# A two-layer graph network on one core: prologue and tail rearranged

## What is computed

```
h = relu(layernorm(x))
Wh = h @ W.T + b_W ;  s_s = Wh @ a_src ;  s_d = Wh @ a_dst
e  = leaky_relu(s_s[src] + s_d[dst] + a_b)          # softmax of e over the edges of one dst
h' = sum over edges of attn * Wh[src]  +  h @ res_W.T + res_b
x  = x + gru(h', h)                                  # layer 0
h  = relu(layernorm(x))
4 times:  a[dst] += W_edge[type] @ h[src] + b_edge[type] ;  h = gru(a, h)
x  = x + h
```

## Time and profile before

| | us |
|---|---|
| median of 3 runs | 586.27 |
| all runs | 581.45 to 586.57 |
| the profiled execution | 584.53 |
| its span on the core | 582.7 |
| busy: PE, DVE, ACT, POOL | 478.6, 267.2, 183.3, 34.2 |

### The profile page before, as it was taken

The page is one execution under the profiler, slowest core; times in us unless marked ns, Lnnn a source line. Parts: engine busy times, 40 slices in busy tenths (PEclk is TensorE's granted clock), DMA queues, the critical chain, the costliest instruction groups (busy, mean ns, idle before and its releaser), DMA issues.

```text
span 582.7 us, 9927 instructions
## 1 busy us (share of the span) xinstructions
PE 478.6 (82%) x3672; PEld 385.0 (66%) x3672; DVE 267.2 (46%) x618; ACT 183.3 (31%) x291; POOL 34.2 (6%) x50
## 2 busy tenths in 40 slices
PE   0146887687777779779659999899998999999995
PEld 0024453454555559769338889788997889888893
DVE  6793888888888883204720122302222122302224
ACT  0042005546576675213241222212222122312221
POOL 2560010000001100000100000000000000000000
PEclk9998988899999999979759999999999999999998
DMA  6000000000000000000000000000000000000001
GB/s 159 1 0 0 1 0 1 2 1 1 1 2 1 1 1 3 3 3 1 0 5 1 0 1 2 1 1 1 1 1 3 1 1 1 1 1 1 1 1 44
DMA packets 5846, 3.65 MB, mean 6 GB/s; under 512 B 499, under 2 KB 5640, under 8 KB 5796
## 3 DMA queue, kind: packets, MB, share of 16 engines
q1 hardware_dynamic: 3188, 1.76, 1.2%
q10 hardware_dynamic: 2608, 1.19, 0.8%
HBM read 2.31 MB, written 0.64 MB: 5 GB/s over the span
## 4 chain that ended last, share of the span: by engine, by line
PE 62%; DVE 19%; issue 7%; DVEq 5%; ACT 3%; POOL 2%; DMA 1%; SPq 0%; POOLq 0%; ACTq 0%
PE big L1259 29%; DVE cell_hot L717 6%; PE small L1269 6%; PE big L1038 4%; PE big L1080 4%; DVE exp_a L756 2%; DVE absent L739 2%; DVEq L254 2%; PE small L1148 2%; PE small L1142 2%; PE small L1146 2%; PE small L1147 2%; PE small L1144 2%; PE small L1143 2%; ACT hn L398 1%
## 5 line engine op out<-in xcount | busy, mean ns | idle before, releaser
L1259 PE MATMUL big<-nibbles,store 128*128 128x256 fp8e4 (+1 forms) x1624 | 180.2, 272 | 6.7 <-DVE store L910 3.4
L1259 PEld LDWEIGHTS big<-nibbles,store 128*128 128x128 f16 x1624 | 159.5, 99 | 25.3 <-issue 7.5
L1038 PE MATMUL big<-cell_hot,store 128*128 128x320 bf16 x420 | 77.9, 321 | 26.1 <-DVE cell_hot L717 25.3
L717 DVE TENSOR_SCALAR cell_hot<-iota,cell_w,fields 128x640 bf16<-128x640 f16 x210 | 77.7, 440 | 19.4 <-PEq L1109 8.7
L1038 PEld LDWEIGHTS big<-cell_hot,store 128*128 x420 | 36.3, 103 | 67.4 <-issue 54.4
L565 ACT ACTIVATE store<-big 128x1024 f32<-128x1024 f32 x20 | 20.5, 1025 | 106.3 <-PE big L1259 106.3
L910 DVE SCALAR_TENSOR_TENSOR store<-small,store 128x256 f16<-128x256 f32 x20 | 8.5, 424 | 91.3 <-ACT store L570 91.1
L806 DVE SCALAR_TENSOR_TENSOR store<-store 128x256 f32<-128x256 f32 x25 | 10.6, 425 | 76.0 <-ACT store L511 76.0
L1269 PE MATMUL small<-store,wT 128*128 128x256 f32 x160 | 37.8, 379 | 0.0
L509 ACT ACTIVATE store<-small,gb 128x256 f32<-128x256 f32 x22 | 10.4, 474 | 73.4 <-PE small L1148 73.4
L1269 PEld LDWEIGHTS small<-store,wT 128*128 128x128 f32 x160 | 28.8, 190 | 3.2
...
## 6 DMA issues: line engine op xcount, KB each, us to landing
...
```

The lines of the kernel that those rows point to most:

```text
L717: last = v.tensor_scalar(cell_hot[:, slot], iota[:], cell_w[:, half, bass.ds(tile + slot, 1)], fields[:, 1, bass.ds(tile + slot, 1)], ALU. ...
L1038: last = mm(big[:, 2 * half + b, 0:HALF], lane_hot[:, bass.ds(tile + slot, 1)].rearrange("p a l -> p (a l)"), cell_hot[:, slot, b * HALF:( ...
L1259: last = mm(big[:, q + t // 2, (t % 2) * CH:(t % 2) * CH + w], h16[parity][:, i, part], A8[:, t % 2, i, c * CH:c * CH + w, t // 2], start= ...
```

## The change

- `Wh` and the destination scores come from one product of each feature tile with `w_gat` (W turned, and one more column W^T a_dst), the bias added by a matmul of one row. The constants are folded from `proj`. The source scores (`score_rows`) are made by PE after the first window.
- All weights are transposed in the prologue, before the features, and ACT copies them before its `hn`.
- `var_e` and all `cell_w` are made by DVE; POOL keeps the power. `bn_stats` is put ahead of the `table`.
- `table` holds one number per window (first tile and number of tiles); "tiles before" is summed in registers. DVE loads the registers of two windows after `weigh`, no longer before it.
- The matmul that ends a window has 2 columns, not 320.
- `degrees`: block 0 after the last window, block 1 before the flag, block 2 before the last two `nodes_turn`, blocks 3 to 9 after the first GRU. The check of the counts comes before the last `weigh`, and the last two turns move across the branch.

```diff
-        def edge_tiles(eng, j):
-            return (eng.value_load(table[0:1, 0, j:j + 1]),
-                    eng.value_load(table[0:1, 1, j:j + 1]),
-                    eng.value_load(table[0:1, 2, j:j + 1], min_val=0, max_val=SLOTS))
+        def edge_tiles(eng, j, ahead):
+            word = eng.value_load(table[0:1, j:j + 1], min_val=0, max_val=256 * (ETP + 1))
+            first, tiles = eng.snap(word & 255), eng.snap(word >> 8)
+            return (first, tiles, ahead), eng.snap(ahead + tiles)
...
-            return big[0:TYPES, 2 + n // 4 % 2]
+            return big[0:TYPES, (2, 1, 0)[(n + 2) // 4]]
...
-            def window_cells(j, half):
-                if later(j, 2):
-                    pool.wait_ge(K.window, j - 1)
-                g.tensor_tensor(cell_w[:, half], fields[:, 2],
-                                base_w[:, bass.ds(j, 1)].to_broadcast([P, ETP]), ALU.subtract).then_inc(K.cellw, 1)
...
-                g.tensor_tensor(var_e[:], mv[:, :, 1], eps[:], ALU.add).then_inc(S0.var, 1)
                 pool.wait_ge(S0.var, r + 1)
...
-            pool.wait_ge(S0.fields, 2)
-            for j in range(NW):
-                window_cells(j, j % 2)
...
-            def weights(k):
+            act.wait_ge(S0.w_T, 1)
...
+            act.wait_ge(S0.proj_ps, 1)
+            a.copy(proj[:], psA[:, 0:4]).then_inc(S0.proj, 1)
+            act.wait_ge(S0.proj, 1)
+            act.wait_ge(L.ab, 16)
+            a.copy(w_gat[:, P:P + 1], proj[:, 1:2])
+            a.activation(dst_bias[:], proj[:, 3:4], ACT.Identity, bias=ab_col[:, 0:1])
+            a.activation(a_rows[:], ones[:], ACT.Copy, scale=proj[:, 0:1]).then_inc(S0.folded, 1)
+            for k in range(4):
                 act.wait_ge(S0.w_T, 2 + k)
-                a.copy(wT[:, 2 + 4 * k:6 + 4 * k], big[:, k % 2].rearrange("p (m o) -> p m o", o=P)
-                       ).then_inc(S0.w_sb, 1)
-            act.wait_ge(S0.w_T, 1)
...
+            turn(0)
             act.wait_ge(S0.s_ps, 1)
...
+            a.activation(s_rows[:], smallf[:, 0:NP], ACT.Identity, bias=proj[:, 2:3]).then_inc(S0.s_rows, 1)
+            for J in range(1, NT + 2):
                 turn(J)
-            weights(0)
-            weights(1)
-            degrees(0, 4)
-            turn(NT + 1)
...
-            degrees(8, 10)
+            degrees(0, 2)
...
             with act.If(1 - flag):
+                turn(NT + 2)
                 first_cells(lambda: attn_out(NT - 1, NT - 1))
+            degrees(2, 6)
+            degrees(6, 10)
...
             link(v.tensor_tensor(tmp_i[:, 1], tmp_i[:, 1], tmp_i[:, 2], ALU.bitwise_or))
             v.scalar_tensor_tensor(fields_r[:, 2], win_r, float(CELLS), tmp_i[:, 1], ALU.mult, ALU.add)
...
...
+                if j >= 2:
+                    dve.wait_ge(K.pair, ends[j - 2])
+                v.tensor_scalar(cell_w[:, half], fields[:, 2], -float(CELLS * j), None, ALU.add).then_inc(K.cellw, 1)
+            variances(0)
+            dve.wait_ge(S0.best_T, 1)
...
+            link(v.tensor_scalar(rg_f[:, 1], down, -1.0, 2.0 * P, ALU.mult, ALU.add))
...
             dve.wait_ge(S0.fields, 2)
...
                 v.tensor_tensor(lane_hot[:, k:k + part],
                                 iota[:, 0:P].unsqueeze(1).to_broadcast([P, part, P]),
                                 fields[:, 0, k:k + part].unsqueeze(2).to_broadcast([P, part, P]),
                                 ALU.is_equal).then_inc(S0.lanes, 1)
-                if k == 0:
...
-                link(v.tensor_tensor(gb[:, l, 0:2], bcol[:, gi:gi + 2], bcol[:, gh:gh + 2], ALU.add))
...
+                for l, (gi, gh) in enumerate(((B_GI, B_GH), (B_IH, B_HH))):
+                    link(v.tensor_tensor(gb[:, l, 0:2], bcol[:, gi:gi + 2], bcol[:, gh:gh + 2], ALU.add))
...
+            def next_range(j):
+                if j < NW:
+                    ranges[j], ends[j] = edge_tiles(dve, j, ends[j - 1])
             def turn(J):
                 if there(J):
                     one_hots(2 * J, 0, ranges[2 * J])
                 if there(J - 1):
                     read_digits(J - 1)
-                for j in (2 * J + 1, 2 * J + 2):
-                    if j < NW:
-                        ranges[j] = edge_tiles(dve, j)
+                if there(J + 1):
+                    window_cells(2 * J + 2, 0)
                 if there(J - 2):
                     weigh(J - 2)
+                next_range(2 * J + 1)
+                next_range(2 * J + 2)
                 if there(J):
                     one_hots(2 * J + 1, 1, ranges[2 * J + 1])
                 if there(J - 1):
                     row_max(J - 1, J - 1)
+                if there(J + 1):
+                    window_cells(2 * J + 3, 1)
                 if there(J - 3):
                     reciprocals(J - 3)
-            ranges = {0: edge_tiles(dve, 0)}
+            dve.wait_ge(S0.table, 1)
+            ranges, ends = {}, {-1: 0}
...
+                if J == 0:
+                    gate_biases()
             dve.wait_ge(K.counted, NT)
...
             with dve.If(1 - flag):
+                turn(NT + 1)
...
-            pe.wait_ge(S0.table, 1)
-            pe.wait_ge(S0.fields, 2)
...
+                pe.wait_ge(s, 16)
+            for k in range(4):
+                for m in range(4):
+                    last = t_.transpose(big[:, k, m * P:(m + 1) * P], wn[:, 2 + 4 * k + m], ident[:])
+                last.then_inc(S0.w_T, 1)
+            pe.wait_ge(S0.bias_sb, 1)
+            pe.wait_ge(S0.b_cols, 1)
+            mm(psA[:, 0:2], wn[:, W_GAT], bcol[:, A_SRC:A_DST + 1], start=True, stop=True, skip_group_check=True)
+            mm(psA[:, 2:4], b_cols[:], bcol[:, A_SRC:A_DST + 1], start=True, stop=True,
...
-            pe.wait_ge(S0.w_sb, 1)
-            for lo, hi in spans():
-                last = mm(smallf[:, lo:hi], wT[:, W_GAT], hT[:, lo:hi], start=True, stop=True)
-            last.then_inc(S0.WhT_ps, 1)
-            pe.wait_ge(S0.WhT, 1)
-            pe.wait_ge(S0.bias_sb, 1)
+            pe.wait_ge(S0.folded, 1)
...
-                mm(psD[:, i:i + 1], WhT[:, i * P:(i + 1) * P], bcol[:, A_DST:A_DST + 1], start=True, stop=True,
-                   skip_group_check=True)
-            pe.wait_ge(S0.a_rows, 1)
...
-            last.then_inc(S0.s_ps, 1)
...
-                last = t_.transpose(smallf[:, i * P:(i + 1) * P], WhT[:, i * P:(i + 1) * P], ident[:])
...
+                o = small[:, i // 3, i % 3 * (P + 1):(i % 3 + 1) * (P + 1)]
+                mm(o, hT[:, i * P:(i + 1) * P], w_gat[:], start=True, stop=False, skip_group_check=True)
+                last = mm(o[:, 0:P], ones[0:1, :], brow[B_W:B_W + 1], start=False, stop=True, skip_group_check=True)
+            last.then_inc(S0.Wh_ps, 1)
...
+            def score_rows():
+                pe.wait_ge(S0.Wh, 1)
+                pe.wait_ge(S0.s_dst, 1)
+                for lo, hi in spans():
+                    last = mm(smallf[:, lo:hi], a_rows[:], hT[:, lo:hi], start=True, stop=True)
+                last.then_inc(S0.s_ps, 1)
...
-                    last = mm(big[:, 2 * half + b, 0:HALF], zero16[:, 0:P], zero16[:], start=False, stop=True,
+                    last = mm(big[:, 2 * half + b, 0:2], zero16[:, 0:P], zero16[:, 0:2], start=False, stop=True,
...
+                else:
+                    pe.wait_ge(S0.s_rows, 1)
...
-                    window(2 * J, 0, edge_tiles(pe, 2 * J))
+                    next_window(2 * J, 0)
+                if J == 0:
+                    score_rows()
...
-            pe.wait_ge(C.const, 7 + TYPES)
-            pe.wait_ge(S0.Wh, 1)
-            pe.wait_ge(S0.s_dst, 1)
...
+            pe.wait_ge(S0.w_sb, 5)
...
-            for s in (L.w2, L.w3, L.w4, L.w5, L.w6):
-                pe.wait_ge(s, 16)
-            weights(0)
-            weights(1)
-            count_turn(NT - 1)
-            aggregate(NT - 3)
-            degrees(0, 4)
-            prob_turn(NT - 2, NT)
-            weights(2)
-            weights(3)
-            degrees(4, 8)
-            aggregate(NT - 2)
+            degrees(0, 1)
+            turn(NT)
             pe.wait_ge(V.total, 1)
-            pe.wait_ge(S0.w_sb, 4)
             mm(big[:, 0, 0:2], ones[:], total[:], start=True, stop=True,
                skip_group_check=True).then_inc(V.total_ps, 1)
-            prob_turn(NT - 1, NT)
-            degrees(8, 10)
+            aggregate(NT - 2)
+            degrees(1, 2)
...
-            def first_cells(after_first):
+            def first_cells(before_first, after_first):
                 residual(0)
                 residual(1)
-                pe.wait_ge(K.degsb, 3)
-                pe.wait_ge(K.probsb, NT)
+                before_first()
+                pe.wait_ge(K.degsb, 1)
                 for c in range(NCH):
                     gates(0, c, c, c % 2, back=2 * (c >= 2))
                     if c == 0:
                         after_first()
+                        pe.wait_ge(K.probsb, NT)
                     if c + 2 < NCH:
```

(5 more changed lines are left out.)

142 lines of the change are left out of this document (70 added, 72 removed).

## The result

The changed kernel took **556.0 us** (median of 4 runs, 555.5 to 556.6), the kernel before beside it 585.8: ratio 0.951, 95% interval 0.946 to 0.955. Forecast were 551.2 us and a range of 544 to 561. Both spans are of one profiled execution, 582.7 and 554.5 us. The table cuts them at the same five events (the end of the last window is that of its last product with `cell_hot`); "sum" is the shift so far.

What follows compares the result with a forecast made beforehand. It saw everything decided in the first 300 us, bound by prologue chains, then DVE in the windows, then PE in the tail. Terms -13.3 - 0.7 - 9.4 - 21 + 11.1 = -33.3 from 584.53 gave 551.2 us, range 544 to 561.

Steps and rivals of the forecast that it cites:

- Part 1: Prologue: first window product at 43.3 us against 56.62, -13.3 us, with DVE's first `cell_hot` at 42.0.
- part 3: Turns 1 to 9: fewer loads, placed behind a multiplication, remove the 1.80 us pause before `weigh`; -9.4 us.
- part 4: Last window to first gates: 320 degree matmuls, weight transposes and a wait leave PE's path; -21 us.
- part 5: Behind the first GRU: degree blocks 3 to 9 stand in front of everything; +11.1 us.
- C: Rival: cheaper tail, PE stays at 2.4 GHz into the steps and part 4's waits are short; 546 us, chance 0.08.
- E: Rival: slower than before, PE left at 1.2 GHz in the four steps; 596 us at 90 us of it, chance 0.03.
- F: Rival: prologue's gain not kept, an unseen wait holds PE before the features; part 1 gives -3, 561 us, chance 0.04.
- A: Rival: in the turns DVE's loads stay open, not hidden under the multiplication; +11, 562 us, chance 0.08.
- D: Rival: degrees come back whole behind the GRU, at clock 0.50 with cold transposes; +6, 557 us, chance 0.07.
- Rival B: Prologue becomes PE's and ACT's, the folding chain takes until `Wh` later than 42; +3 to +5, 555 us, chance 0.1.
- part 2: First two windows: `score_rows` replaces a wait for DVE's loads, and the gate biases hide behind it; -0.7 us.
- 0.25 comes back: In each turn, two loads and entering the window loop exceed the multiplication of 1.49 us by 0.25 us.

Runs made afterwards that it cites:

- b_nobias: The changed kernel without the bias `b_W` in `Wh` (ten one-row products left out, so its output differs); 556.3 us, ratio 0.949.
- i_rows128: The changed kernel with the bias of `Wh` added by full weight tiles (128 rows of 1/128) instead of one-row tiles; 553.9 us, ratio 0.945.
- c_gb: The changed kernel with the gate biases made by DVE behind the last turn instead of behind the first; 557.9 us, ratio 0.952.
- d_loads: The changed kernel with DVE's two register loads of a turn ahead of `weigh` again; 560.3 us, ratio 0.956.
- l_six: The changed kernel with six register loads per turn on DVE instead of two, at the changed kernel's place; 586.0 us, ratio 1.000.
- f_degfront: The changed kernel with all ten blocks of degrees ahead of the verdict's flag again; 563.3 us, ratio 0.961.
- j_pool2: The changed kernel with `cell_w` of windows 2 to 19 on POOL, DVE keeping its waits with a memset behind; 556.0 us, one run.

## Why the prediction was near, and what in it was wrong

**Right.** Part 1's DVE side (41.62 for 42.0), part 3 (-9.0 to the last full `weigh` against -9.4), part 4 in its first profile (-20.5 against -21, with both waits named; seven of nine later profiles make it some 19, so there is luck in that match), the order of part 5, the four steps. Rivals C, E and F did not happen; A did not either, the bracket ahead of `weigh` is gone. Of D there is a part: the degrees ran at the upper rate, but the transposes behind them did not.

**Rival B happened in part, 2 us.** The step that failed is "twenty matmuls of 129 columns ... take 5 to 10 by clock". They took 14.6. The price came from products that all had full weight tiles; ten of the twenty have one row. Without them the first window product comes 2.7 (b_nobias) and 1.7 us (i_rows128) earlier than in the profile after, and DVE ends the prologue as forecast. That the granted clock was 0.50 from 22 us on explains only a part: mostly at that rate, ten full products took 4.0.

**"The biases of the gates (1 us on DVE) hide behind it" was wrong, 1.2 to 1.4 us at their place.** They stood behind the second window, where DVE was late, not behind the product of `score_rows`; without them (c_gb) the third window starts that much earlier after the first product, of which 0.3 was left at the first `weigh`. With that and nothing gained on balance at the first windows, part 2 came to +0.2 (the first `read_digits` comes 11.15 earlier, the first product 11.33) and not to -0.7.

**Part 3 had the right size, and more of it is the number of loads than their place.** It counted on the cover of the multiplication, and rival A on its failing. Moving the loads back (d_loads) costs only 0.2 a turn, since two loads leave 0.54 at the old place where six left 1.80; their number carries the gain, and l_six (four reads more, 3.1 us a turn) has the same sign. The forecast of "0.25 comes back" was met by the 0.32. Its 1.2 for two reads with gaps is right too: they come each 0.62 on the sequencer. Only the gaps must not be forgotten, as l_six's expectation did.

**Part 5 was 1.3 too cheap.** The 1.1 for a clock kept up by the degrees did not come: the granted clock is 1.00 under them and until 264, then it falls, to 0.50 from 266 to 278, while PE is busy for 5.47 of the 10 us up to 272. The first transposes of `hn` and the first `gather` take what they took before. The kernel before:

```profile
293.97 1.51 PE L1245 MATMUL small<-ident,hn 128*128 128x128 f32 x6 [2.35 <-ACT hn L398]
...
300.69 5.28 PE L1259 MATMUL big<-nibbles,store 128*128 128x256 fp8e4 x24 [3.27 <-issue]
```

The changed kernel, where the `gather` of 272.18 above has the same 5.28:

```profile
265.43 1.54 PE L1263 MATMUL small<-ident,hn 128*128 128x128 f32 x6
```

So neither the 0.5 for faster transposes nor the 1.1 was gained; the degrees themselves took 0.6 less than the 16.4 of the forecast. f_degfront's 13.4 and 26.0 differ by 12.6, so the whole +12.4 is the place of the degrees.

Of the 5.1 us missing (28.2 of 33.3 in the spans), 2.0 are the one-row products, 1.3 the windows (0.9 the first two with the gate biases, 0.4 the turns), 0.2 tail and GRU, 1.3 part 5 and 0.3 the four steps. The tail is the least certain: later executions have 1.5 to 2 us more there.

The two rules that were weighed: the lock between DVE and POOL (SBUF — State Buffer, section "SBUF: two separate sides", of the Trainium skill) did not show beside the power: by it the one-hots would have started near 21, and they started at 19.32. Beside POOL's subtraction it shows in part: in j_pool2 `exp_a`, which reads two tiles in SBUF, takes 0.26 longer (1.74 for 1.48). The floor of about 600 ns for `tensor_load` (the Trainium skill, DMA: Bandwidth & Descriptors, section "Latency and other measured facts") is not that of the instruction, 0.306 here, but one read with its arithmetic and gaps takes 0.62. The measured rows decide: the loads without arithmetic in the kernel before (180.1, 180.5, 180.8) come 0.3 to 0.4 apart.
